# A new merge order for three streams of steps on four engines of a fused language-model tower

## What is computed

```python
h = tok(x, itok)              # LN(word + pos + type), gated mix with a projected word vector
h = h + attn0(layernorm(h))   # 12 heads, causal, weighted sums of k v^T, norm per head, Wo
h = h + ffn0(layernorm(h))    # router picks 19 of 128 tokens for attention, the rest get a
                              # pooled mix; then LN, gelu(n2 @ W1 + bf1) @ W2 + bf2
h = h + attn1(layernorm(h))   # 12 heads of 16, softmax over 128
h = h + moe(layernorm(h))     # 8 experts, top 2 of a softmax gate, 192 -> 768 -> 192
```

## Time and profile before

| | |
|---|---|
| median of 3 runs | 1018.1 us (1016.38 to 1019.54) |
| the profiled execution | 1015.77 us, span 1014.0 us |
| mean granted TensorE clock | 0.829 |
| TensorE busy | 797.5 us (79%) |
| VectorE busy | 531.0 us (52%) |
| ScalarE busy | 273.0 us (27%) |
| GpSimd busy | 240.2 us (24%) |

### The profile page before, as it was taken

How to read it: one execution, slowest core, us unless ns; L and a number is a source line. 1 busy time by engine, 2 the same in 40 slices (tenths; PEclk the granted TensorE clock), 3 DMA queues, 4 the chain that set the end, 5 groups by cost and what they waited for, 6 DMA issues and landing times.

```text
span 1014.0 us, 16268 instructions
## 1 busy us (share of the span) xinstructions
PE 797.5 (79%) x5452; PEld 615.2 (61%) x5453; DVE 531.0 (52%) x1769; ACT 273.0 (27%) x494; POOL 240.2 (24%) x303
## 2 busy tenths in 40 slices
PE   2556488989787979778798977877763899999994
PEld 2336365647575555667445666735542899999993
DVE  4655587636677663668575457741244333333331
ACT  0122232524242343333161442321321111111110
POOL 3403014410013630003252001320003033333332
PEclk9967689979577898868598976768755799999998
DMA  7920000000001100000120000074012122122220
GB/s 234 417 101 7 1 1 21 2 1 3 1 1 48 24 1 1 2 1 24 33 15 1 2 1 1 32 199 121 1 46 77 25 41 35 32 39 33 32 33 8
DMA packets 30115, 42.97 MB, mean 42 GB/s; under 512 B 5335, under 2 KB 24357, under 8 KB 30046
## 3 DMA queue, kind: packets, MB, share of 16 engines
q1 hardware_dynamic: 19684, 30.59, 9.5%
q0 software_dynamic: 8752, 9.07, 5.6%
q10 hardware_dynamic: 1610, 2.40, 0.7%
HBM read 20.64 MB, written 22.09 MB: 42 GB/s over the span
## 4 chain that ended last, share of the span: by engine, by line
issue 41%; PE 31%; POOL 12%; DVE 7%; DMA 3%; ACT 2%; DVEq 1%; SPq 1%; another core or an unknown queue 1%; POOLq 0%; ACTq 0%
PE qa L1787 17%; PE qc L1787 11%; POOL slots L527 3%; PE qc L1790 3%; POOL arena_w L440 3%; PE qa L1790 2%; DMA out<-qk_T 1%; POOL arena_b L510 1%; POOL tk L466 1%; DMA tok_no<-in_tok_no 1%; POOL hb L488 1%; POOL rs_a L474 1%; POOL tk L463 1%; DVE arena_w L1415 1%; DMA arena_w<-in_word_emb,idx_cur 1%
## 5 line engine op out<-in xcount | busy, mean ns | idle before, releaser
L1787 PE MATMUL qc<-arena_w,big 128*128 x468 | 83.1, 328 | 1.4 <-DVE qk_T L1767 1.4
L996 ACT ACTIVATE big<-qa 128x768 f32<-128x768 f32 x39 | 31.6, 810 | 192.8 <-PE qc L1787 168.1
L1787 PE MATMUL qa<-xT,arena_b 97*128 97x128 f32 (+1 forms) x624 | 77.9, 282 | 4.5 <-DVE arena_b L1760 2.5
L1787 PEld LDWEIGHTS qa<-xT,arena_b 97*128 97x128 f32 (+1 forms) x624 | 73.9, 195 | 11.1 <-issue 11.1
L1753 DVE COPY xT<-qc 96x256 f32<-96x256 f32 x39 | 16.4, 421 | 118.7 <-PE qc L1790 118.7
L1787 PEld LDWEIGHTS qc<-arena_w,big 128*128 128x128 f32 x468 | 75.6, 191 | 2.0 <-issue 2.0
L1415 DVE TENSOR_REDUCE arena_w<-qc 128x6 f32<-128x768 f32 x28 | 25.7, 952 | 77.4 <-PE qc L1787 77.4
L609 POOL DMA_INDIRECT out<-qk_T x39 | 60.9, 1563 | 21.6 <-POOL spare L608 12.7
L1787 PE MATMUL qa<-w_l,nT 96*128 96x384 f32 (+1 forms) x128 | 52.9, 579 | 0.0
L1787 PE MATMUL qc<-qk_T 17*128 17x128 f32 (+2 forms) x680 | 38.0, 356 | 14.2 <-DVE qk_T L1421 10.7
L1790 PE MATMUL qa<-cst,arena_b 128*128 128x128 f32 (+2 forms) x232 | 38.1, 309 | 12.7 <-DVE arena_b L1229 7.3
(11 more groups left out here) (350 smaller groups left out, 1679.8 us busy)
## 6 DMA issues: line engine op xcount, KB each, us to landing
slots<-xk SPq DMA_DIRECT2D x1, 13192.0 KB, 40.6
arena_e<-in_w SPq DMA_DIRECT2D x8, 576.0 KB
arena_w<-in_w SPq DMA_DIRECT2D x8, 576.0 KB, 9.9
qk_T<-slots SPq DMA_DIRECT2D x39, 97.0 KB
...
out<-qk_T POOLq DMA_INDIRECT x39, 3.5
...
```

The source lines that it names most:

```text
L996: A(hTm[:, u % 2, :, :].rearrange("p (c j) t -> p c (j t)", c=2), PS[u % 2][:, :, 0:384], ACT.Gelu).then_inc(m_gelu, 1)
L1787: return nc.tensor.matmul(o, l, r, start=start, stop=stop)
```

## The change

No step is added, removed or altered, and no wait either: in the lists of `front` on GpSimd, ScalarE and VectorE and in those of `joint` on all four engines the steps of the three streams are put into another order relative to each other. Within a stream each engine keeps its order. TensorE's list of `front`, all of `back` and the expert tiles stay as they are. The indentation is cut, and steps that stay in place are left out where several follow each other.

GpSimd, `front` and `joint`:

```diff
@@ -533,43 +533,43 @@
     carry(3).then_inc(s["keep"], 1)
...
 def front(ta):
-    next_words(ta + 1)
     scale_k(ta, 0)
...
     scale_k(ta, 3)
+    next_words(ta + 1)
     next_vectors(ta + 1)
-    token_root(ta + 1)
     root_front(ta, "ln2", 11)
     root_front(ta, "ln3", 3)
+    token_root(ta + 1)
     scale_token(ta + 1, 0)
...
     root_back(tb, "ln4")
-    next_words(ta + 1)
     residual(tb, 0)
-    next_vectors(ta + 1)
     residual(tb, 1)
-    token_root(ta + 1)
     residual(tb, 2)
     residual(tb, 3)
+    next_words(ta + 1)
+    root_back(tb, "ln5")
+    next_vectors(ta + 1)
+    scale_k(ta, 0)
+    scale_k(ta, 1)
+    token_root(ta + 1)
+    scale_k(ta, 2)
     scale_token(ta + 1, 0)
-    scale_k(ta, 0)
+    scale_k(ta, 3)
     scale_token(ta + 1, 1)
-    root_back(tb, "ln5")
-    scale_k(ta, 1)
-    scale_k(ta, 2)
-    scale_k(ta, 3)
     root_front(ta, "ln2", 11)
...
     scatter(tb, 1)
+    scatter_done(tb)
     ln1_root(ta + 1)
-    scatter_done(tb)
...
     root_back(tb, "ln4")
```

ScalarE, `front` (first piece) and `joint`:

```diff
@@ -851,10 +851,10 @@
     q_evac(ta)
...
     word_vectors(ta + 1)
-    token_gate(ta + 1)
     route_exp(ta, 0)
...
     route_exp(ta, 2)
+    token_gate(ta + 1)
     route_exp(ta, 3)
...
     pT_evac(ta, 1)
@@ -866,26 +866,23 @@
     x1T_evac(ta, 1)
...
     vug_evac(ta, 1)
+    n4T_evac(tb, 0)
+    n4T_evac(tb, 1)
     vug_evac(ta, 2)
+    ffn_gelu(tb, 0)
+    ffn_gelu(tb, 1)
+    ffn_gelu(tb, 2)
     vug_evac(ta, 3)
...
     squares(ta, 1)
+    ffn_gelu(tb, 3)
+    ffn_gelu(tb, 4)
     squares(ta, 2)
-    n4T_evac(tb, 0)
-    n4T_evac(tb, 1)
+    ffn_gelu(tb, 5)
     squares(ta, 3)
-    ffn_gelu(tb, 0)
-    ffn_gelu(tb, 1)
     gates_exp(ta)
-    ffn_gelu(tb, 2)
-    ffn_gelu(tb, 3)
     qk_roots(ta)
-    ffn_gelu(tb, 4)
-    ffn_gelu(tb, 5)
     score_exp(ta)
-    qk_evac(ta, 0, 0)
-    qk_evac(ta, 0, 1)
-    qk_evac(ta, 0, 2)
     x5T_evac(tb, 0)
...
     qk1_evac(tb, 0)
@@ -893,7 +890,10 @@
     qk1_evac(tb, 2)
...
     qk1_evac(tb, 4)
+    qk_evac(ta, 0, 0)
     qk1_evac(tb, 5)
+    qk_evac(ta, 0, 1)
+    qk_evac(ta, 0, 2)
     v1_evac(tb, 0)
...
     qk_evac(ta, 1, 0)
@@ -902,25 +902,25 @@
     ob_evac(ta, 0)
...
     exps(tb, 0, 1)
+    qk_evac(ta, 2, 0)
     o_evac(tb, 0)
-    qk_evac(ta, 2, 0)
     qk_evac(ta, 2, 1)
...
     exps(tb, 1, 0)
+    exps(tb, 1, 1)
     qk_evac(ta, 3, 0)
     qk_evac(ta, 3, 1)
-    exps(tb, 1, 1)
+    o_evac(tb, 1)
     qk_evac(ta, 3, 2)
     ob_evac(ta, 2)
-    o_evac(tb, 1)
     ob_evac(ta, 3)
+    head_roots(ta)
     exps(tb, 2, 0)
     exps(tb, 2, 1)
-    head_roots(ta)
-    o_evac(tb, 2)
     onT_evac(ta, 0)
     onT_evac(ta, 1)
+    o_evac(tb, 2)
     exps(tb, 3, 0)
...
     n3T_evac(ta, 0)
@@ -928,22 +928,22 @@
     router_exp(ta)
...
     scores_evac(ta)
+    kT_evac(ta)
     x6T_evac(tb, 0)
     x6T_evac(tb, 1)
-    kT_evac(ta)
+    gate_softmax(tb)
     v2_evac(ta, 0)
-    gate_softmax(tb)
     v2_evac(ta, 1)
...
     pselT_evac(ta)
-    gates_evac(tb)
     word_vectors(ta + 1)
...
     route_exp(ta, 3)
+    gates_evac(tb)
     pT_evac(ta, 0)
...
     asel_evac(ta, 0)
```

VectorE, `front` (first piece and half of the second) and `joint`:

```diff
@@ -1514,7 +1514,6 @@
 def front(ta):
...
     rope(ta, 1)
-    token_stats(ta + 1)
     rope(ta, 2)
...
     prior_dot(ta, 0)
@@ -1541,79 +1540,81 @@
     spread(ta, 2, True)
...
     head_norm(ta)
+    token_stats(ta + 1)
     attn_out(ta, 0)
...
     ln_3(ta)
+    token_apply(ta + 1)
     router_dot(ta)
...
     pool_weights(ta)
-    token_apply(ta + 1)
     ranks(ta)
...
     head_queries(ta, 1)
-    token_dot(ta + 1)
     route_max(ta, 0)
     route_max(ta, 1)
+    token_dot(ta + 1)
+    mixed(ta, 0)
     token_diff(ta + 1)
-    mixed(ta, 0)
     mixed(ta, 1)
     route_norm(ta, 0)
+    token_mix(ta + 1)
     route_norm(ta, 1)
     mix_in(ta, 0)
-    token_mix(ta + 1)
+    ln1_stats(ta + 1)
     mix_in(ta, 1)
...
     contexts(ta, 1)
-    ln1_stats(ta + 1)
     ln1_apply(ta + 1)
...
     ln4_stats(tb)
+    rope(ta, 0)
     ln4_apply(tb)
-    rope(ta, 0)
     rope(ta, 1)
     rope(ta, 2)
-    token_stats(ta + 1)
     rope(ta, 3)
...
     qk_norms(ta)
-    token_apply(ta + 1)
+    token_stats(ta + 1)
+    ffn_out(tb, 0)
     score_max(ta)
+    ffn_out(tb, 1)
+    ln5_stats(tb)
+    ln5_apply(tb)
     coefficients(ta)
...
     scale_q(ta, 1)
-    ffn_out(tb, 0)
-    ffn_out(tb, 1)
-    ln5_stats(tb)
-    ln5_apply(tb)
     mask(ta, 0, 0)
+    maxima(tb, 0, 0)
     mask(ta, 0, 1)
-    maxima(tb, 0, 0)
+    scale_q(ta, 2)
     maxima(tb, 0, 1)
-    scale_q(ta, 2)
     below(tb, 0)
     spread(ta, 0)
+    token_apply(ta + 1)
     mask(ta, 1, 0)
     mask(ta, 1, 1)
+    scale_q(ta, 3)
     attend(tb, 0)
-    scale_q(ta, 3)
     maxima(tb, 1, 0)
+    token_dot(ta + 1)
     maxima(tb, 1, 1)
+    spread(ta, 1)
     below(tb, 1)
-    spread(ta, 1)
     mask(ta, 2, 0)
     mask(ta, 2, 1)
+    attend(tb, 1)
     spread(ta, 2)
-    attend(tb, 1)
     mask(ta, 3, 0)
...
     maxima(tb, 2, 0)
@@ -1622,14 +1623,13 @@
     spread(ta, 3)
...
     attend(tb, 2)
-    token_dot(ta + 1)
-    maxima(tb, 3, 0)
     attn_out(ta, 0)
-    maxima(tb, 3, 1)
     attn_out(ta, 1)
     ln2_stats(ta)
+    maxima(tb, 3, 0)
+    maxima(tb, 3, 1)
+    ln2_apply(ta)
     below(tb, 3)
-    ln2_apply(ta)
     ln_3(ta)
...
     router(ta)
@@ -1638,8 +1638,8 @@
     ln6_stats(tb)
...
     ranks(ta)
+    gate_max(tb)
     selection(ta)
-    gate_max(tb)
     top_two(tb)
...
     pooled(ta)
@@ -1647,23 +1647,23 @@
     head_queries(ta, 1)
...
     route_max(ta, 0)
+    token_diff(ta + 1)
     route_max(ta, 1)
     mixed(ta, 0)
-    token_diff(ta + 1)
     mixed(ta, 1)
...
     route_norm(ta, 1)
-    token_mix(ta + 1)
     mix_in(ta, 0)
     mix_in(ta, 1)
+    token_mix(ta + 1)
     contexts(ta, 0)
...
     rows_out(tb, 0)
+    selected_in(ta, 0)
+    ln1_apply(ta + 1)
+    selected_in(ta, 1)
     rows_out(tb, 1)
-    ln1_apply(ta + 1)
-    selected_in(ta, 0)
-    selected_in(ta, 1)
...
     ln4_stats(tb)
```

TensorE, `joint`:

```diff
@@ -2192,43 +2192,43 @@
     x1_T(ta, 1)
...
     proj(ta, 1)
-    proj(ta, 2)
-    proj(ta, 3)
-    prior_sums(ta, 0)
     n4_T(tb, 0)
     n4_T(tb, 1)
+    proj(ta, 2)
+    ffn_up(tb, 0)
+    proj(ta, 3)
+    ffn_up(tb, 1)
+    prior_sums(ta, 0)
     prior_sums(ta, 1)
-    prior_sums(ta, 2)
-    prior_sums(ta, 3)
-    ffn_up(tb, 0)
-    ffn_up(tb, 1)
     ffn_up(tb, 2)
...
     ffn_up(tb, 5)
+    prior_sums(ta, 2)
+    prior_sums(ta, 3)
+    ffn_down(tb, 0)
+    ffn_down(tb, 1)
+    ffn_down(tb, 2)
     scores_T(ta)
-    ffn_down(tb, 0)
-    scores_back(ta)
-    ffn_down(tb, 1)
-    cumulate(ta)
-    ffn_down(tb, 2)
     ffn_down(tb, 3)
-    qk_turn(ta, 0, 0)
-    qk_turn(ta, 0, 1)
-    qk_turn(ta, 0, 2)
-    kq(ta, 0)
     x5_T(tb, 0)
...
     qk1(tb, 0)
+    scores_back(ta)
     qk1(tb, 1)
+    cumulate(ta)
     qk1(tb, 2)
...
     qk1(tb, 4)
+    qk_turn(ta, 0, 0)
+    qk_turn(ta, 0, 1)
     qk1(tb, 5)
     v1_rows(tb, 0)
+    qk_turn(ta, 0, 2)
     v1_rows(tb, 1)
+    kq(ta, 0)
+    logits(tb, 0)
     qk_turn(ta, 1, 0)
-    logits(tb, 0)
     qk_turn(ta, 1, 1)
...
     av(ta, 0)
@@ -2240,33 +2240,33 @@
     qk_turn(ta, 2, 0)
...
     qk_turn(ta, 2, 1)
+    qk_turn(ta, 2, 2)
     logits(tb, 1)
-    qk_turn(ta, 2, 2)
     av(ta, 1)
+    ob_T(ta, 1)
     max_T(tb, 1)
-    ob_T(ta, 1)
     kq(ta, 2)
...
     qk_turn(ta, 3, 2)
+    av1(tb, 1)
     av(ta, 2)
-    av1(tb, 1)
+    o_T(tb, 1)
     ob_T(ta, 2)
-    o_T(tb, 1)
     kq(ta, 3)
...
     logits_T(tb, 2)
-    av1(tb, 2)
-    o_T(tb, 2)
     on_T(ta, 0)
     on_T(ta, 1)
+    av1(tb, 2)
+    wo(ta, 0)
+    o_T(tb, 2)
+    wo(ta, 1)
     logits(tb, 3)
-    wo(ta, 0)
-    wo(ta, 1)
     max_T(tb, 3)
...
     n3_T(ta, 0)
@@ -2275,31 +2275,31 @@
     o_T(tb, 3)
...
     keys(ta)
+    values(ta, 0)
     x6_T(tb, 0)
     x6_T(tb, 1)
-    values(ta, 0)
     gate(tb)
...
     queries(ta)
+    counts(tb)
     select_T(ta)
-    counts(tb)
-    gates_T(tb)
     words_T(ta + 1)
     route_logits(ta, 0)
+    word_vectors(ta + 1)
     route_logits(ta, 1)
-    bias_rows(tb, 0)
-    word_vectors(ta + 1)
     mix(ta, 0)
...
     probs_T(ta, 0)
+    gates_T(tb)
     probs_T(ta, 1)
+    bias_rows(tb, 0)
     context(ta, 0)
-    bias_rows(tb, 1)
     context(ta, 1)
...
     attn(ta, 0)
+    bias_rows(tb, 1)
     attn(ta, 1)
...
```

## The result

The changed kernel took 1033.7 us (median of 1031.76 to 1039.41) against 1018.7 us for the kernel before in the same comparison: ratio 1.018, 95% interval 1.0141 to 1.0219. It is slower, by 15 us between the medians and by 18 by the ratio; the forecast was 1020, in a range of 1004 to 1035. The profiled execution took 1031.8 us (span 1029.9), mean granted clock 0.818.

The account below looks back on a forecast made before the run. TensorE's in-order queue was taken to set the pass, its idle time and clock being what order can win. Three passes at +2.2 us (+6.6) and front -4.7 gave +1.9 on the 1018.1 median: 1020.0 us, range 1004 to 1035.

Parts of the forecast that it names:

- rival 2: Attention stretch around 412: clock falls earlier, +4.5 to +5.5 us a pass on top of +2.2, 1034 us; chance 0.18.
- first part: Pass up to `logits(0)`: TensorE idles 4.9 us in place of 6.8, so -1.9 us a pass.
- masks: Between `logits(0)` and the first `max_T`: two masks more on VectorE, +1.6 us a pass, 0 if TensorE is late anyway.
- token steps: `token_apply` ahead of `mask(1)` +0.3, `token_dot` and `scale_q(3)` ahead of second `maxima(1)` +1.8: +2.1 us a pass.
- tail: End of a pass: +0.6 us at the wait before the mix, +1.0 between mix and `context`; its other moves 0.
- Front: `prior_sums` start at 56.0 and take 0.5 us a pair; less losses behind, -4.7 us, bounds -7 and 0.
- That one long wait is no worse than scattered ones: At `x5_T`: by the clock rule, the longer single wait is no worse than six scattered ones; danger lies at 412.
- on_T and wo: `on_T` into the wait after `logits_T(2)`, `wo` ahead of `logits(3)`: -2.6 us a pass; longer ln2 chain +1.4.
- `word_vectors` and `token_diff`: Before the mix: `route_max(1)` delayed, `token_diff` no longer last; TensorE's 1.29 us wait grows by 0.6.
- `gates_T` and `bias_rows`: Between mix and `context`: they leave a place with slack, and ScalarE's copy is only half hidden, +1.0 us a pass.

Follow-up runs that it names:

- the middle: Kernel before with only the attention's middle in the new order (`logits(1)` behind `qk_turn(2,2)`, `max_T(1)` behind `ob_T(1)`), token steps left in place: 1000.5 us, ratio 0.9995.
- The gates' move: Kernel before with only `gates_T` and `bias_rows(0)` moved into the `probs_T` stretch, `bias_rows(1)` and `gates_evac` moved later: 999.9 us, ratio 0.9967.
- VectorE's: Kernel before with only VectorE's tail moves: `token_diff` ahead of `route_max(1)`, `token_mix` behind `mix_in(1)`, `ln1_apply` between the `selected_in`, `rows_out(1)` last: 1007.8 us, ratio 1.0066.

## Why the prediction was wrong

The failed step is the sum of a pass. Each move was priced as a delay at the speed of the row beside it, and what a move does to TensorE's clock was put at nothing in the sum of a pass; only rival 2 had it. The traces of the changed kernel and of the kernel before on the later chips, means of three passes, show by stretch what came instead:

| stretch of a pass | forecast, us | measured, us |
|---|---|---|
| start to `logits(0)` (first part) | -1.9 | -0.4 |
| to the first `max_T` (masks) | +1.6 | +1.8 |
| to `max_T(1)` (token steps) | +2.1 | +4.3 |
| to `n3_T` (`on_T`, `wo`, ln2) | -1.2 | -0.4 |
| to `mix` (tail) | +0.6 | +3.2 |
| to the end (tail) | +1.0 | +1.5 |
| a pass | +2.2 | +9.9 |

In the first comparison the same sum is +4.1; 3.5 us of the difference lie between `mix` and the end of the pass, where the kernel before had the holds.

- **Front.** The term was right: `prior_sums` at 56.94 us and 0.49 us a pair, and the first `x1_T` at 157.6 against 162.2, 4.5 us where I had 4.7. The time of the front alone gained 8.2 (4.8 to 11.6), more than the stage shows. In the first comparison it read +4.9; of the 8.5 us by which the two traces of the changed kernel differ at `x1_T`, 6.6 are there at `on_T`, behind the holds.
- **First part.** In the run of it alone `logits(0)` comes 1.9 us earlier, as forecast. But the longer wait at `x5_T` kept the clock at 1.2 GHz for two `qk1` of 3.78 us and part of the third, to about 393, where before the window of 382 to 387 was the last. That one long wait is no worse than scattered ones was wrong by some 2 to 3 us at `qk1`; in the changed kernel only 0.4 us of the gain was left.
- **Masks.** +1.6 forecast, +1.8 measured: right.
- **Token steps.** +2.1 a pass forecast, +2.4 in the time when moved alone, and `max_T(1)` 2.0 us later. The term was right; taken as a sum with the others it failed, and the middle's own 1.4 us there had no term.
- **on_T and wo.** Net -1.2 a pass forecast; alone -4.2 by the time, but -1.0 by the traces. Whether the term was too small stays open.
- **Tail.** The largest miss in the table, and 6.2 us a pass by itself, against +0.6 for `word_vectors` and `token_diff` and +1.0 for `gates_T` and `bias_rows`. The gates' move and VectorE's are worth -1.1 and +2.2 alone and 4.1 together. I priced each as a delay; together they let TensorE's clock fall between `mix` and the end of the pass, and in the changed kernel it is down at `values(1)` too (2.4 to 2.9 us for 1.55). I applied the clock only to the one place where the trace of before already showed it fall.
- **Rival 2.** Mechanism and place right: clock down at 417, 79 us into the pass, behind a stretch with TensorE busy 3.05 of 5 us, as it said, `kq(2)` 2.93 us for 1.61, `max_T(1)` late by 5.0 in that pass and not 2. Its price of 4.5 to 5.5 a pass fits: first part, middle and tokens together cost 6.2 a pass, 5.0 more than their sum one by one. It gave 1034 and 1033.7 came. That agreement is partly luck: what the tail costs above its 1.6 us was missing in it, and the holds in the kernel before stand against that.
- I had given it 0.18. What should have weighed more: every inserted step there acts twice, as a delay and as idle time of TensorE.
